# A prologue in finer steps, and a last projection by tiles, in a gated-attention and feed-forward kernel

## The chip, the cores and the metric

The kernel runs on one core of one Trainium2 chip. The metric is device time in microseconds (us), the median of some runs. A core has TensorE (PE, matrix products), VectorE (DVE), ScalarE (ACT), GpSimd (POOL) and SyncE (SP, which only starts transfers here). In the profile, matrix products show as MATMUL on PE with a weight load beside them (PEld); a product of fp32 operands shows as two instructions. PSUM, the memory that PE writes, has eight banks: ps_f has four and ps_a has four.

## The reference

16 sequences of 256 tokens, 256 wide, go through one layer of gated attention (an mLSTM in parallel form) and one feed-forward part of four layers.

```python
x = x + xattn(layernorm(x), ctx, ctx)      # q = normed x, k = v = ctx, 8 heads of 32
x = x + ffn(layernorm(x))

def xattn(q, k, v):
    pre = 15 * tanh((concat(q, k, v) @ ifgate_w.T + ifgate_b) / 15)     # 8 i-gates, 8 f-gates
    lf = cumsum(log_sigmoid(f_pre))
    log_d = lf[t] - lf[s] + i_pre[s], masked to t >= s;  m = rowmax(log_d)
    s_mat = (q k^T / sqrt(32)) * exp(log_d - m)
    h = s_mat v / (max(|rowsum(s_mat)|, exp(-m)) + 5e-5)
    return h * rsqrt(mean(h^2) + 1e-6) * (1 + outnorm_w)
def ffn(x):                                 # 256 -> 1024 -> 1024 -> 1024 -> 256, weights -1, 0, 1 with scales
    h = silu(x @ w1) * (x @ w2); h = gelu(h @ h1); h = gelu(h @ h2); return h @ w3
```

## The kernel before

The 16 sequences are worked through in 8 pairs (W = 2, so Q = 4 tiles of 128 tokens). A loop `batch(i)` on every engine does three things at once. It runs the feed-forward part of pair i. It runs the second half of the attention of pair j = i + 1 (masks, scores, values, residual, second norm). And it runs the first half for pair g = i + 2 (norm, turn, gates, scans). Each product of the feed-forward part is split into a high and a low part, so PE gets two passes (L1185 and L1186 for the first layer, L1209 and L1210 for the two hidden ones, L1242 and L1243 for the last).

What the loop overlaps has to be done in the open ahead of it: the whole attention of pair 0 and the first half of pair 1. This is the prologue, written out by hand at the end of each engine's program. Its order decides everything, since each engine takes its instructions in order and waits on semaphores. The steps, with the names that they have in the code:

- `norm_1_stats`, `norm_rsqrt`, `norm_1_apply` (DVE): mean and variance, then the root by integer seed and three Newton steps (eleven short linked instructions, L667 to L672), then z in four tiles (L693).
- `turn_z` (PE, L1036): 8 transposes of z into PSUM; `take_zT` (ACT, L510) copies them out.
- `plain_gates_keys` and `plain_gates_normed` (PE, L1059): gate products; `soft_cap` (tanh) and `softplus` (exp, ln) on ACT; between them an activation table is loaded (ACT_TABLE_LOAD).
- `scan_f`, `scan_m` (DVE): running sums and maxima over the 16 rows of gates. `spread_maxima` (PE, L1076) copies each of the 16 rows of maxima to all 128 partitions by a product that contracts over those 16 rows; `turn_rows` (L1106) turns the gate rows, `take_cols` (ACT) takes them out.
- `masks` (DVE, L776), `decays` (ACT, exp), `scores` (PE, L1128), `weigh_scores` (DVE, L792), `make_state` (L1137), `values` (PE, L1148: 8 heads of 33 columns each), `read_state` (L1158), `take_far`, `take_num`.
- `mix_divide`, `mix_square`, `mix_rsqrt`, `residual` (DVE), then the second norm (L678 to L693), `turn_z2` (L1036), `take_z2T` on ACT (z2_hi, L573) and on DVE (z2_lo, L872), and the first product of the feed-forward part (L1185).
- `keep_clock(n)` (PE, L1316) issues n products of no use, so that PE stays busy.

In the prologue the gates of pair 1 are worked out before pair 0's scores, with rows of pair 1 held in spare parts of z. POOL issues nine weight loads (11 MB), six ahead of `weigh_keys(0)` and three behind it. At the end `project` gives the last layer: two PSUM banks, each with both tiles of a sequence; `finish` (DVE) scales (L900) and adds (L906) a sequence at a time, and one transfer of 512 KB (L352) stores a pair. `decide` (L925) then sets a flag by which every engine skips a general path.

## Time and profile before

| | |
|---|---|
| median of 3 runs | 841.72 us (840.33 to 843.19) |
| the profiled execution's own time | 841.54 us |
| its span, first to last instruction | 839.7 us |
| PE busy, of the span | 97% |
| DVE, ACT, POOL busy | 66%, 45%, 6% |
| first feed-forward product starts | 80.94 us |
| last feed-forward product starts | 832.10 us |
| mean granted TensorE clock | 0.972 |

Times of instructions are us from the start of the span. The granted clock (PEclk) is 1.00 at 2.4 GHz and 0.50 at 1.2 GHz. A line of the timeline gives the start, the time that the merged instructions took, the engine, the line, the operation and the tiles, and in brackets the idle time before it and what ended it.

### The profile page before, as it was taken

The numbers are of one execution on the slowest core, as the hardware profiler recorded it, in microseconds if no ns is written. First come the engines' busy times: TensorE is split into PE (matmuls) and PEld (weight loads), VectorE is DVE, ScalarE is ACT, GpSimd is POOL, SyncE is SP. The second block draws the span as 40 slices with busy tenths as digits, with TensorE's granted clock in tenths as the row PEclk, the third lists the DMA queues.
The fourth block names the chain that finished last, engine by engine and source line by source line (L and its number), as shares of the span: only waits on it lengthen the run. The fifth ranks groups of instructions, "written<-read, shape, count | busy, mean of one in ns | idle before, by whom it ended". The sixth has DMA issues, their size and how long they took to land.

```text
span 839.7 us, 11914 instructions
## 1 busy us (share of the span) xinstructions
PE 816.1 (97%) x4666; PEld 693.7 (83%) x4666; DVE 558.1 (66%) x1335; ACT 375.9 (45%) x546; POOL 47.7 (6%) x53
## 2 busy tenths in 40 slices
PE   8895999999999999999999999999999999999996
PEld 7694788888888888888888888888888888888885
DVE  5656785758685695858666595947857583865543
ACT  2301554546345562455545462355535463336331
POOL 3100002000020001100020001100020000000000
PEclk9657999999999999999999999999999999999999
DMA  9804000040012200040002200131000300350540
GB/s 340 352 2 176 1 26 27 26 176 1 26 52 101 76 26 27 25 159 18 27 26 94 108 26 12 41 127 51 26 27 30 147 1 1 125 172 5 164 137 27
DMA packets 14027, 63.24 MB, mean 75 GB/s; under 512 B 1952, under 2 KB 2320, under 8 KB 11152
## 3 DMA queue, kind: packets, MB, share of 16 engines
q1 hardware_dynamic: 12672, 50.91, 17.4%
q0 software_dynamic: 1296, 11.53, 3.5%
q8 instruction: 38, 0.62, 0.3%
q14 instruction: 21, 0.17, 0.1%
HBM read 53.94 MB, written 8.50 MB: 74 GB/s over the span
## 4 chain that ended last, share of the span: by engine, by line
PE 78%; DVE 12%; issue 1%; ACT 1%; DVEq 0%; ACTq 0%
PE ps_f L1209 22%; PE ps_f L1210 22%; DVE decay L776 7%; PE ps_f L1185 7%; PE ps_f L1186 7%; PE ps_a L1148 6%; PE ps_f L1242 4%; PE ps_f L1243 4%; DVE decay L792 2%; PE ps_a L1128 2%; PE ps_a L1036 2%; PE ps_a L1137 1%; PE ps_a L1158 1%; PE ps_a L1099 1%; PE ps_a L1092 1%
## 5 line engine op out<-in xcount | busy, mean ns | idle before, releaser
L1209 PE MATMUL ps_f<-h_hi,wgt 128*128 128x512 f32 x1024 | 404.1, 395 | 0.0
L1210 PE MATMUL ps_f<-h_lo,wgt 128*128 128x512 f32 x1024 | 399.1, 390 | 0.0
L1209 PEld LDWEIGHTS ps_f<-h_hi,wgt 128*128 128x128 f32 x1024 | 192.4, 188 | 40.3 <-issue 0.5
L1210 PEld LDWEIGHTS ps_f<-h_lo,wgt 128*128 128x128 f32 x1024 | 192.4, 188 | 38.0
L890 DVE TENSOR_TENSOR h_lo<-work,h_hi 128x512 fp32r<-128x512 f32 x128 | 86.5, 690 | 135.0 <-ACT h_hi L596 134.0
L591 ACT ACTIVATE work<-ps_f,scl 128x512 f32<-128x512 f32 x128 | 87.5, 683 | 161.4 <-PE ps_f L1210 161.2
L1185 PE MATMUL ps_f<-h_hi,wgt 128*128 128x512 f32 x256 | 101.4, 396 | 0.1
L1186 PE MATMUL ps_f<-h_lo,wgt 128*128 128x512 f32 x256 | 100.4, 392 | 0.0
L578 ACT ACTIVATE work<-ps_f,scl 128x512 f32<-128x512 f32 x64 | 44.1, 688 | 92.6 <-PE ps_f L1186 92.6
L596 ACT ACTIVATE h_hi<-work 128x512 fp32r<-128x512 f32 x128 | 80.9, 632 | 4.0
L881 DVE SCALAR_TENSOR_TENSOR work<-ps_f,scl,work 128x512 f32<-128x512 f32 x64 | 48.1, 751 | 49.2 <-ACT work L578 49.2
L776 DVE SCALAR_TENSOR_TENSOR decay<-decay,cols,future 128x128 f32<-128x128 f32 x224 | 64.5, 364 | 0.0
L1242 PE MATMUL ps_f<-wgt,h_hi 128*128 128x256 f32 x256 | 62.2, 285 | 0.0
L1148 PEld LDWEIGHTS ps_a<-v_aug,decay 128*128 128x128 f32 x480 | 60.7, 201 | 1.6
L1243 PE MATMUL ps_f<-wgt,h_lo 128*128 128x256 f32 x256 | 61.8, 283 | 0.0
L1185 PEld LDWEIGHTS ps_f<-h_hi,wgt 128*128 128x128 f32 x256 | 48.0, 188 | 15.1 <-DVE work L881 3.7
L1148 PE MATMUL ps_a<-v_aug,decay 128*128 128x33 f32 x480 | 59.1, 280 | 0.0
L1186 PEld LDWEIGHTS ps_f<-h_lo,wgt 128*128 128x128 f32 x256 | 48.1, 188 | 8.8
L557 ACT ACTIVATE decay<-decay 128x1024 f32<-128x1024 f32 x32 | 33.9, 1060 | 42.8 <-DVE decay L776 42.8
L1243 PEld LDWEIGHTS ps_f<-wgt,h_lo 128*128 128x128 f32 x256 | 49.1, 192 | 0.1
L1242 PEld LDWEIGHTS ps_f<-wgt,h_hi 128*128 128x128 f32 x256 | 49.1, 192 | 0.1
L886 DVE TENSOR_TENSOR h_lo<-work,h_hi 128x512 fp32r<-128x512 f32 x64 | 43.7, 683 | 0.8
(156 smaller groups left out, 764.5 us busy)
## 6 DMA issues: line engine op xcount, KB each, us to landing
decay<-m_rows SPq DMA_DIRECT2D x14, 1024.0 KB, 6.1
decay<-w_cols SPq DMA_DIRECT2D x22, 512.0 KB, 4.2
wgt<-w_cols POOLq DMA_DIRECT2D x5, 1024.0 KB, 13.7
v_aug<-ctx_tok SPq DMA_DIRECT2D x8, 528.0 KB, 3.6
xs<-x SPq DMA_DIRECT2D x8, 512.0 KB, 3.6
wgt<-w_cols POOLq DMA_DIRECT2D x2, 2048.0 KB, 10.0
x_kept<-xs SPq DMA_DIRECT2D x8, 512.0 KB, 2.7
out<-xs SPq DMA_DIRECT2D x8, 512.0 KB, 2.6
```

What stands on the lines that cost most here:

```text
L591: act.activation(work[:, m % GELU], ps_f[:, (turn_of(i) + m) % 4], ACT.Gelu, scale=scl[:, 2 + layer, m:m + 1]).then_inc(s_gelu, 1)
L596: act.activation(h_hi[1 - layer][:, m], work[:, m % GELU], ACT.Copy).then_inc(s_hi, 1)
L776: last = dve.scalar_tensor_tensor(part, maxima, cols[:, t, row:row + 1], future[:], ALU.subtract, ALU.add)
L881: dve.scalar_tensor_tensor(work[:, 2 + m % 2], ps_f[:, bank], scl[:, 1, m:m + 1], work[:, m % 2], ALU.mult, ALU.mult).then_inc(s_hf, 1)
L890: dve.tensor_tensor(h_lo[1 - layer][:, m], work[:, m % GELU], h_hi[1 - layer][:, m].bitcast(F32), ALU.subtract).then_inc(s_lo, 1)
L1148: last = pe.matmul(value_out(j, b, t)[:, h * DV:(h + 1) * DV], decay_of(b, h, t), v_aug[:, b * TILES + t, h, :], start=True, stop=True)
L1185: pe.matmul(ps_f[:, bank + half], w, moving(z2_hi[:, c], as_is), start=(c == 0), stop=False)
L1186: last = pe.matmul(ps_f[:, bank + half], w, moving(z2_lo[:, c], as_is), start=False, stop=(c == CH - 1))
L1209: pe.matmul(ps_f[:, bank], w, moving(h_hi[layer][:, k], as_is), start=(k == 0), stop=False)
L1210: last = pe.matmul(ps_f[:, bank], w, moving(h_lo[layer][:, k], as_is), start=False, stop=(k == KH - 1))
L1242: pe.matmul(to, moving(h_hi[0][:, k, q * P:(q + 1) * P], as_is), w, start=(k == 0), stop=False)
L1243: last = pe.matmul(to, moving(h_lo[0][:, k, q * P:(q + 1) * P], as_is), w, start=False, stop=(k == KH - 1))
```

## The change

- First norms and turns of pair 0 go tile by tile: x comes in four transfers, each transposed tile follows its z tile, and the copies to zT, z2_hi and z2_lo are made in halves, which the gates and the first feed-forward products wait for one by one.
- The three roots of the prologue are exp(-0.5 ln v) on ACT (`root`), with one Newton step on DVE (`newton`), instead of eleven DVE steps.
- `spread_maxima` contracts over all 128 rows of state, cleared beforehand, and signals after each pair of heads.
- The values of a sequence are started when two of its four row groups are weighed (`first_values`). The second pair's turn, gates and scans come behind the first pair's values; `turn_rows(1)` and `take_cols(1)` come inside `batch(0)`.
- `split_gate_weights` and the gain go from DVE to POOL; gate_w and ctxT(0) are loaded from ACT's queue; two of the six weight loads that were ahead of `weigh_keys(0)` go behind it.
- The last pair's projection has a bank for each tile, and `finish_last` and `store_last` go by tiles.

```diff
+            for q in range(Q):
+                sp.dma_start(xs[0][:, q], x[0][:, q]).then_inc(s_x_first[q], 16)
...
+            def store_last(i):
+                for q in range(Q):
+                    b, t = q // TILES, q % TILES
+                    if t:
+                        sp.wait_ge(s_y, W * i + b + 1)
+                    else:
+                        sp.wait_ge(s_tail_y, b + 1)
+                    sp.dma_start(out[i][:, q], xs[i % 2][:, q]).then_inc(s_out if q == Q - 1 else s_tail_out[q], 16)
...
-            load_weights((0, 1, 2, 3, 4, 5))
+            load_weights((0, 1, 2, 3))
             weigh_keys(0)
-            load_weights((6, 7, 8))
+            load_weights((4, 5, 6, 7, 8))
+            split_gate_weights()
+            pool.wait_ge(s_gain, 16)
+            pool.tensor_scalar(gain_b[:], gain_b[:], 1.0, None, ALU.add).then_inc(s_gain, 1)
...
+            def root(n, logs, v, y):
+                act.wait_ge(s_var, n + 1)
+                act.activation(logs, v, ACT.Ln).then_inc(s_log, 1)
+                act.wait_ge(s_log, n + 1)
+                act.activation(y, logs, ACT.Exp, scale=-0.5).then_inc(s_root, 1)
...
+            act.dma_start(gw_in, gate_w).then_inc(s_gw, 16)
+            act.dma_start(ctxT(0), ctx_t[0]).then_inc(s_ctxT[0], 16)
+            act.preload_act_table_set("natural_log_exp_and_others")
+            root(0, nw[:, 1, 0:Q], nw[:, 0, 0:Q], nw[:, 3, 0:Q])
             act.preload_act_table_set("exp_and_others")
             take_zT(0)
             act.wait_ge(s_gb, 1)
             soft_cap(0)
+            act.wait_ge(s_cleared, 2)
             softplus(0)
-            act.preload_act_table_set("exp_and_others")
-            take_zT(1)
             take_cols(0)
             decay_cols(0)
             decays(0, 0)
+            decays(0, 1)
+            take_near(0)
+            take_zT(1)
+            root(1, rms[:, 1, 0:Q * HEADS], rms[:, 0, 0:Q * HEADS], rms[:, 3, 0:Q * HEADS])
+            act.preload_act_table_set("exp_and_others")
             soft_cap(1)
-            decays(0, 1)
             softplus(1)
-            take_near(0)
-            take_cols(1)
-            act.wait_ge(s_layer_const, 32)
+            root(2, nw[:, 1, 0:Q], nw[:, 0, 0:Q], nw[:, 3, 0:Q])
+            act.preload_act_table_set("silu_and_others")
             take_z2T(0)
+            act.wait_ge(s_scl, 16)
...
+            def newton(tile, n):
...
+                link(s_lead, 0, dve.tensor_tensor(prod, y, y, ALU.mult))
+                link(s_lead, 0, dve.scalar_tensor_tensor(prod, prod, -0.5, v, ALU.mult, ALU.mult))
+                link(s_lead, 0, dve.scalar_tensor_tensor(y, prod, 1.5, y, ALU.add, ALU.mult))
+            def first_norm_stats(src, landed):
+                for q in range(Q):
+                    if landed:
+                        dve.wait_ge(s_x_first[q], 16)
+                    last = dve.bn_stats(stats[:, q], src[:, q])
+                link(s_lead, 0, last)
+                for q in range(Q):
+                    last = dve.bn_aggr(mv[:, q], stats[:, q])
+                link(s_lead, 0, last)
+                dve.tensor_scalar(nw[:, 0, 0:Q], mv[:, :, 1], LN_EPS, None, ALU.add).then_inc(s_var, 1)
+            def first_norm_apply(root, src, dst, done):
+                dve.wait_ge(s_root, root + 1)
+                newton(nw, Q)
+                for q in range(Q):
+                    dve.tensor_scalar(dst[:, q], src[:, q], mv[:, q, 0:1], nw[:, 3, q:q + 1], ALU.subtract, ALU.mult).then_inc(done, 1)
+                dve.wait_ge(done, Q)
...
+            def first_num(b):
+                if b == 0:
+                    dve.wait_ge(s_gw_split, 4)
+                dve.wait_ge(s_far, 1)
+                dve.wait_ge(s_pv, TILES * (b + 1))
+                dst = num[:].rearrange("p (b t e) -> p b t e", b=W, t=TILES)[:, b, 1]
+                far = state[:].rearrange("p (b n) -> p b n", b=W)[:, b]
+                added = dve.tensor_tensor(dst, value_out(0, b, 1), far, ALU.add)
+                if b:
+                    added.then_inc(s_num, 1)
+                    dve.wait_ge(s_num, 1)
+                else:
+                    link(s_lead, 0, added)
+            def first_square(b):
+                n = TILES * HEADS
+                at = slice(b * n, (b + 1) * n)
+                sq = h_sq.rearrange("p (n d) -> p n d", d=DH)[:, at]
+                if b:
+                    dve.wait_ge(s_near, 1)
+                else:
+                    dve.wait_ge(s_near_first, 1)
+                link(s_lead, 0, dve.tensor_tensor(sq, heads[:, at, 0:DH], heads[:, at, 0:DH], ALU.mult))
+                link(s_lead, 0, dve.tensor_reduce(rms[:, 2, at], sq, AX.X, ALU.add))
+            def first_mix():
+                total = heads[:, :, DH]
+                dve.wait_ge(s_floor, 1)
...
+                dve.tensor_scalar(rms[:, 0], rms[:, 2], RMS_EPS, None, ALU.add).then_inc(s_var, 1)
+                dve.wait_ge(s_root, 2)
+                newton(rms, Q * HEADS)
+                link(s_lead, 0, dve.tensor_tensor(den[:, 0], rms[:, 3], den[:, 1], ALU.mult))
...
+            def finish_last(i):
+                for q in range(Q):
+                    b, t = q // TILES, q % TILES
+                    at, bank = slice(t * DIM, (t + 1) * DIM), (turn_of(i) + q) % 4
+                    dve.wait_ge(s_ymm, Q * i + q + 1)
+                    scaled = dve.tensor_tensor(y_tmp[:, b, at], ps_f[:, bank, 0:DIM], w3s_b[:], ALU.mult)
+                    if t:
+                        scaled.then_inc(s_ysc, 1)
+                        dve.wait_ge(s_ysc, W * i + b + 1)
+                    else:
+                        scaled.then_inc(s_tail_scaled, 1)
+                        dve.wait_ge(s_tail_scaled, b + 1)
+                        dve.wait_ge(s_x1kept, 16 * i + 16)
+                    kept = resident(i)[:, q]
+                    dve.tensor_tensor(kept, y_tmp[:, b, at], kept, ALU.add).then_inc(s_y if t else s_tail_y, 1)
...
-            norm_1_stats(0)
-            norm_rsqrt(s_norm1, 0)
-            norm_1_apply(0)
+            dve.memset(state[:, 0:2 * SEQ], 0.0).then_inc(s_cleared, 1)
+            first_norm_stats(xs[0], True)
+            first_norm_apply(0, xs[0], z, s_z_first)
             dve.wait_ge(s_const, 16)
             dve.tensor_scalar(gb[:], gb_in[:], 1.0 / CAP, None, ALU.mult).then_inc(s_gb, 1)
             norm_1_stats(1)
             norm_rsqrt(s_norm1, 1)
+            scan_f(0)
+            shift_g(0)
+            scan_m(0)
             norm_1_apply(1)
-            scan_f(0)
-            scan_m(0)
             dve.wait_ge(s_ident, 8)
-            masks(0)
+            masks(0, (0,))
+            masks(0, (1,), (0,))
             weigh_scores(0, 0)
+            masks(0, (1,), (1,))
+            floors(0)
+            take_state(0)
             weigh_scores(0, 1)
-            take_state(0)
+            take_far(0)
+            first_num(0)
+            first_square(0)
+            first_num(1)
+            first_square(1)
+            assert count[s_lead] == LEAD_REDUCED, count[s_lead]
+            first_mix()
+            residual(0)
+            first_norm_stats(xs[0], False)
             scan_f(1)
-            scan_m(1)
-            split_gate_weights()
-            floors(0)
-            dve.wait_ge(s_gain, 16)
-            dve.tensor_scalar(gain_b[:], gain_b[:], 1.0, None, ALU.add).then_inc(s_gain, 1)
-            take_far(0)
-            take_num(0)
-            mix_divide(0)
-            mix_square(0)
-            mix_rsqrt(0)
-            residual(0)
-            norm_2_stats(0, xs[0])
-            norm_rsqrt(s_norm2, 0)
-            norm_2_apply(0, xs[0])
+            first_norm_apply(2, xs[0], z2, s_z2_first)
+            shift_g(1)
+            running_max(1)
             take_z2T(0)
-            dve.wait_ge(s_layer_const, 32)
+            offsets(1)
+            dve.wait_ge(s_scl, 16)
...
+            def turn_first(src, ready, half_done, done):
+                for q in range(Q):
+                    pe.wait_ge(ready, q + 1)
+                    for c in range(CH):
+                        last = pe.transpose(ps_a[:, c, q * P:(q + 1) * P], src[:, q, c * P:(c + 1) * P], ident[:])
+                        if q == Q - 1:
+                            last.then_inc(done if c else half_done, 1)
...
-            def spread_maxima(b, heads_of):
-                for h in heads_of:
+            def spread_maxima(b, h0):
+                for h in (h0, h0 + 1):
                     row = b * HEADS + h
-                    last = pe.matmul(spread_out(h), ident[0:BH, row:row + 1].to_broadcast([BH, P]), m_row(0),
+                    last = pe.matmul(spread_out(h), ident[:, row:row + 1].to_broadcast([P, P]), state[:, SEQ:2 * SEQ],
                                      start=True, stop=True)
-                return last
+                last.then_inc(s_spread, 1)
...
+            def first_values(b, part):
+                pe.wait_ge(s_smat, ROWGRP * b + 2 * part + 2)
+                for r in FIRST_WEIGHED[2 * part:2 * part + 2]:
+                    for h in (r, r + ROWGRP):
+                        for t in range(TILES):
+                            last = pe.matmul(value_out(0, b, t)[:, h * DV:(h + 1) * DV], decay_of(b, h, t), v_aug[:, b * TILES + t, h, :],
+                                             start=True, stop=True)
+                last.then_inc(s_pv, 1)
...
+                    if first(i) and m == 2:
+                        turn_rows(1)
...
-            keep_clock(20)
+            keep_clock(14)
             plain_gates_keys(0)
+            turn_first(z, s_z_first, s_zT_first, s_zT)
+            keep_clock(2)
+            plain_gates_normed(0)
+            keep_clock(18)
+            pe.wait_ge(s_scan, 3)
+            pe.wait_ge(s_cleared, 2)
+            spread_maxima(0, 0)
+            turn_rows(0)
+            for h in (2, 4, 6):
+                spread_maxima(0, h)
+            pe.wait_ge(s_mask, 1)
+            for h in (0, 2):
+                spread_maxima(1, h)
+            scores(0, 0)
+            pe.wait_ge(s_mask, 2)
+            for h in (4, 6):
+                spread_maxima(1, h)
+            pe.wait_ge(s_v, 16)
+            first_values(0, 0)
+            make_state(0)
+            first_values(0, 1)
+            scores(0, 1)
+            read_state(0)
+            first_values(1, 0)
+            first_values(1, 1)
+            turn_z(1)
             plain_gates_keys(1)
-            turn_z(0)
-            plain_gates_normed(0)
-            keep_clock(8)
-            turn_z(1)
-            keep_clock(8)
-            pe.wait_ge(s_scan, 3)
+            plain_gates_normed(1)
+            keep_clock(24, 1)
             pe.wait_ge(s_zTe, 2)
-            spread_maxima(0, range(0, 2))
-            pe.wait_ge(s_cleared, 1)
-            turn_rows(0)
-            spread_maxima(0, range(2, 4)).then_inc(s_spread, 1)
-            spread_maxima(0, range(4, 8)).then_inc(s_spread, 1)
-            pe.wait_ge(s_mask, 1)
-            spread_maxima(1, range(0, 4)).then_inc(s_spread, 1)
-            plain_gates_normed(1)
-            pe.wait_ge(s_mask, 2)
-            spread_maxima(1, range(4, 8)).then_inc(s_spread, 1)
-            scores(0, 0)
-            scores(0, 1)
-            make_state(0)
-            values(0, 0, 0)
-            values(0, 1, 0)
-            read_state(0)
-            values(0, 0, 1)
-            values(0, 1, 1)
-            turn_rows(1)
-            keep_clock(24, 1)
-            turn_z2(0)
-            keep_clock(8, 1)
+            turn_first(z2, s_z2_first, s_z2T_first, s_z2T)
+            keep_clock(2, 1)
```

## Rows read from the trace of the kernel before

**Rows 1.** Windows: busy us (instructions) of PE, PEld, DVE, ACT, POOL; granted clock; DMA; GB/s.
```profile
82.00:176.00 94.00, 93.91 (x549) 79.75 (x548) 65.15 (x157) 47.58 (x69) 6.19 (x4) 1.00 0.11 40
```
**Rows 2.** Timeline, first norm, turn and gates of pair 0.
```profile
2.12 7.49 PE L1316 MATMUL ps_f<-ident 128*128 128x128 f32 x40 [2.12 <-POOL ident L469]
8.73 1.38 DVE L693 TENSOR_SCALAR z<-xs,mv,nw 128x256 f32<-128x256 f32 x4
...
15.33 1.93 PE L1059 MATMUL ps_a<-work,num 128*48 128x256 f32 x8 [1.11 <-ACT work L510]
```
**Rows 3.** Timeline, table load, exp and running sum of the first gates.
```profile
17.85 1.28 ACT L531 ACT_TABLE_LOAD   x1
...
19.14 0.42 ACT L535 ACTIVATE state<-rows 16x256 f32<-16x256 f32 x1
...
20.11 0.68 DVE L743 TENSOR_TENSOR_SCAN state<-state 16x256 f32<-16x256 f32 x1 [4.28 <-ACT state L537]
```
**Rows 4.** Timeline, maxima spread, masks, scores weighed, values.
```profile
23.80 7.75 PE L1076 MATMUL ps_f<-state,ident 16*128 16x256 f32 x20
...
25.08 2.37 DVE L776 SCALAR_TENSOR_TENSOR decay<-ps_f,cols,future 128x128 f32<-128x128 f32 x8 [2.17 <-PE ps_f L1076]
...
39.24 2.47 DVE L792 SCALAR_TENSOR_TENSOR decay<-ps_a,decay 128x512 f32<-128x512 f32 x4
...
47.59 0.46 DVE L718 MEMSET gw_split<- 128x480 f32 x1 [0.16 <-issue]
...
52.34 6.88 PE L1148 MATMUL ps_f<-v_aug,decay 128*128 128x33 f32 x32
```
**Rows 5.** Windows cut where the granted clock changes; columns as in the first group.
```profile
22.40:25.00 2.60, 2.51 (x12) 1.91 (x13) 0.47 (x2) 0.65 (x3) 0.33 (x1) 1.00 1.07 433
25.00:31.40 6.40, 6.40 (x16) 4.54 (x14) 4.41 (x16) 2.08 (x2) 2.47 (x5) 0.50 0.85 313
31.40:35.10 3.70, 3.70 (x10) 1.49 (x9) 2.16 (x8) 0.03 (x1) 0.00 (x0) 0.50 1.06 443
...
46.00:50.00 4.00, 4.00 (x20) 4.00 (x21) 2.85 (x14) 0.39 (x1) 0.00 (x0) 0.50 0.02 4
...
62.50:66.50 4.00, 3.93 (x35) 3.74 (x34) 3.52 (x15) 0.00 (x0) 0.00 (x0) 0.99 0.49 164
```
**Rows 6.** Chain that ended last, batch 0: the attention steps amid the feed-forward part.
```profile
111.87 1.17 PE ps_a L1128 x32
...
120.53 0.90 PE ps_a L1137 x8
121.43 1.71 PE ps_a L1148 x16
```
**Rows 7.** Chain that ended last, from the mixing's root to the first feed-forward product.
```profile
64.23 0.19 DVE rms L667
...
66.92 1.24 DVE num L856
...
70.70 1.42 DVE stats L678 x4
...
76.38 1.98 PE ps_a L1036 x8
...
78.44 1.03 ACT h_hi L573
...
79.57 1.24 DVE h_lo L872
...
80.94 0.47 PE ps_f L1185
```
**Rows 8.** The page's transfers: KB each, us from issue to landing.
```profile
decay<-m_rows SPq DMA_DIRECT2D x14, 1024.0 KB, 6.1
```
**Rows 9.** Timeline, the end.
```profile
832.42 0.69 DVE L900 TENSOR_TENSOR num<-ps_f,w3s_b 128x512 f32<-128x512 f32 x1 [1.22 <-PE ps_f L1243]
833.03 1.28 DVE L906 TENSOR_TENSOR xs<-num,xs 128x512 f32<-128x512 f32 x2
...
834.34 0.34 SPq L352 DMA_DIRECT2D out<-xs  x1
```

More of the change, by code:

```diff
@@ L216, in build @@
         s_out = sem("s_out")
+        s_tail_scaled = sem("s_tail_scaled")
+        s_tail_y = sem("s_tail_y")
+        s_tail_out = [sem(f"s_tail_out{n}") for n in range(Q - 1)]
         def first(j):
             return isinstance(j, int) and j == 0
-        def early(j):
-            return isinstance(j, int) and j == 1
         def zT(j):
@@ L394, in _ @@
                         load_raw(n)
-                store(i)
+                    store_last(i)
+                else:
+                    store(i)
+            for n in range(Q - 1):
+                sp.wait_ge(s_tail_out[n], 16)
             sp.wait_ge(s_x1kept, 16 * PAIRS)
@@ L526, in soft_cap @@
                     act.wait_ge(s_gate_sum, j - W + 1)
-                act.activation(rows[0:GATE_COLS], gate_out(j)[0:GATE_COLS] if plain(j) else gate_sum, ACT.Tanh, bias=gb[:], scale=1.0 / CAP).then_inc(s_gact, 1)
+                act.activation(rows[0:GATE_COLS], gate_out[0:GATE_COLS] if plain(j) else gate_sum, ACT.Tanh, bias=gb[:], scale=1.0 / CAP).then_inc(s_gact, 1)
             def softplus(j):
@@ L603, in batch @@
                         hi_1(i, m - 1)
+                    if first(i) and m == 3:
+                        take_cols(1)
                 hi_1(i, KH - 1)
@@ L756, in scan_m, with offsets @@
                 dve.wait_ge(s_scan, n + 3)
+            def offsets(j):
+                f, m = f_row, m_row
+                g = rows[ROW_G:ROW_G + BH]
                 c = m[:, P - 1:P]
@@ L787, in weigh_scores @@
             def weigh_scores(j, b):
-                for r in range(ROWGRP):
+                for r in FIRST_WEIGHED if first(j) else range(ROWGRP):
                     dve.wait_ge(s_qk, W * j + b + 1)
@@ L1244, in part @@
                     return last
+                if final:
+                    for t in range(TILES):
+                        part(0, t, range(KH - 1))
+                    for t in range(TILES):
+                        part(0, t, range(KH - 1, KH)).then_inc(s_ymm, 1)
+                    for t in range(TILES):
+                        part(1, t, range(KH)).then_inc(s_ymm, 1)
+                    return
                 for b in range(W):
```

238 lines of the change are left out of this document (148 added, 90 removed).

## The prediction, made before the changed kernel ran

> **What bounds the kernel now.** I read the page first: one core, PE busy 97% of the span. The windows cut to stretches then say where PE isn't the bound. In a stretch inside the loop PE is busy 93.91 of 94 us at the full clock [rows 1], and the edits hardly touch it. So the change can pay only before the first feed-forward product, at 80.94 [rows 7], and behind the last product of the projection, at 832.1. What lies between is fixed: from 80.94 to the span's end 758.8 us, and 1.8 us more in the execution's own time of 841.5, which is 0.2 us under the median.
>
> The first 80.94 us are a chain through four engines. Three parts of it matter. (1) Up to the gates of pair 0, PE is in the way: 40 products of no use until 9.6, then the key gates, and the gates on normed x end at 17.26 [rows 2]. (2) From 25.1 to 59.2 it is masks, scores and values, and here the granted clock decides. It is 1.00 when the spread of maxima begins and 0.50 from 25.0 [rows 5]. PE is busy without a break from 25.0 to 31.4 with products that contract over 16 rows, and the clock does not come back. It comes back at 35.1, after 3.7 us of gate products over 128 rows [rows 5]. So rows in use count, and busy time alone doesn't. It is low again through the values, where PE is likewise never idle (46 to 50), and high again from 62.5 under useless 128-column products [rows 5]. The price: 16 value instructions take 1.71 us in the loop [rows 6], 32 take 6.88 us here [rows 4], so 3.44 for 16, double. (3) From the last values (59.2) to 80.94 DVE works alone, step by step [rows 7].
>
> **The change, part by part.**
>
> *First gates.* 28 useless instructions take the place of 40. At their mean of 0.187 us they end at 7.4, and at the slower rate of their start near 8.1; I take 8.0. Then 1.93 for the key gates, 1.0 for 8 transposes (1.98 at half clock [rows 7]), so the turn ends at 11.0. The z tiles are no longer in the way: they were ready at 10.1 [rows 2] and come about 1.7 earlier by the short root and the four transfers of x. Half copies of 0.55 (1.03 for the whole [rows 7]) let the first half of the gate products start at 11.6, so they end at 13.6: 3.7 us earlier. Two transfers more on SP's queue and two on ACT's cost some 0.4 each at the start, where these queues have nothing else. The bound on the other side: if the clock rises later, the key gates cost 1.9 more.
>
> *Gates to masks.* Tanh, table load, exp and ln stay as they are: running sum at 20.11 before [rows 3], 16.45 now. The maximum is ready 1.85 later (18.3), offsets 0.9, and `norm_1_apply(1)` (1.4) now stands between them and the masks. Masks start at 20.65, not at 25.08.
>
> *Masks, scores, values.* DVE's work, with eight masks at 2.2 and a weighing at 2.47 [rows 4]: 4.35 for sequence 0, 2.2, weighing 2.5 (ends 29.7), 2.2, floors and state 0.95, weighing 2.5. At full clock PE keeps up: a pair of heads spread in 0.9 (1.9 for 5 instructions at half clock, 7.75 for 20 [rows 4]), so DVE never waits long. The first values start at 28.45, when two row groups are weighed. They take 1.71, state 0.90, values 1.71, scores 1.17 to 1.5 [rows 6], and DVE weighs sequence 1 until 36.85. The last values end at **39.1**. That is the floor. But in this stretch PE has 33-column products and gaps, much as where the clock was low before. What I expect is that the spread, now over 128 rows, holds the clock (as the gate products brought it back), and that it falls amid the first values, near 32. Then the second values, scores, state and last values run at half clock: second values until 33.9, scores 36.0, state read 38.1, two values of 3.44 each until **45.0**. If it falls at 28.4, the last values end at **48.6**. If the 128 rows don't help and it is low from 22 on, every spread pair costs 1.7, masks wait as before, and they end at **53.8**.
>
> *Last values to first feed-forward product* (21.7 us before). Half of the squares is hidden (1.25 off). The mix's root: eleven DVE steps at 0.224 (twelve fill 64.23 to 66.92 [rows 7]), 2.46, become ln and exp on ACT and three steps. No row has a 128x4 or 128x32 ln; below lies 0.4 for both, above the 0.42 each of a 16x256 exp plus three handovers of 0.1 [rows 3], 1.2. I take 0.65, nearer the small end since the elements are few: 1.1 off. The second norm's root is the same, but `scan_f(1)` (0.68) lies in it: 0.9 off. The turn of z2 follows the tiles, at full clock: 1.98 becomes 0.5, 1.5 off. z2_hi (1.03) and z2_lo (1.24) go in halves, the second halves beside the first products, with `running_max(1)` 0.25 in the way: 1.2 off [rows 7]. Sum 6: **15.4 to 15.9** us remain.
>
> What is moved behind the values is pair 1: turn, gates (2 x 1.93 at full, double at half clock), useless products, then on ACT tanh, two table loads, exp, ln. At full clock they are ready 7.7 us after the last values, where DVE wants them at 10.7. If the clock is low they need 9.5 to 12, and `scan_f(1)` and the ACT root behind it wait up to 1.4. That is inside the 15.9.
>
> By the Trainium skill, "ScalarE: Activation LUTs", section "What ACT_TABLE_LOAD costs", a switch takes about 2.66 us, 1.28 of load and 1.38 of drain. Here the load starts at 17.85, takes 1.28, and exp starts at 19.14 [rows 3], so no such drain stands behind it. By the page's figure the second gates would be ready 2.8 us later, and the time would be an estimated 823.5. The sum goes by the row.
>
> *Moved to POOL.* `split_gate_weights` and the gain: DVE had a gap there (memset 0.46 at 47.59 [rows 4]), so nothing is gained, and POOL does them from about 24.5, ahead of the first read at 33. Nothing; at most 1.6 (their time on DVE) if they stood in DVE's way.
>
> *Moved into batch 0.* `turn_rows(1)` on PE and `take_cols(1)` on ACT: 0.5 us on the bound engine. The copy of maxima (6.1 us [rows 8]) has 19 us before the masks of batch 0: hidden. Cost **+0.5**.
>
> *The end.* Before: scale 832.42, two adds, store at 834.34 [rows 9]. The last product ends at the same time. Now a half scale (0.4) and a half add (0.35): store at 833.3. 1.0 off, and 0 to 1.2 for a quarter of the bytes; I take **1.3 off**.
>
> **Sum.** 45.0 + 15.9 = 60.9 for the first product, 20.0 earlier; 841.5 - 20.0 + 0.5 - 1.3 = 820.7, so **821**.
>
> **Rivals.**
> - *The clock holds through the values.* Products start at 39.1 + 15.4 = 54.5, at most 1 us lost if it falls in the pause before the turn: 841.5 - 26.4 + 0.5 - 1.3 = 814.3, or 815. For it: the loop has such values at full clock [rows 1, 6], though among big products. Against: they didn't bring the clock back in 46 to 50 [rows 5]. Chance 0.20.
> - *The clock is low from the start of values, or the second gates come late on top:* 48.6 + 15.8 = 64.4, so 824.2. For it: more pauses in PE than before. Chance 0.22.
> - *The change doesn't do what it says:* the spread over 128 rows counts no more than one over 16, the clock falls near 22. 53.8 + 15.7 = 69.5: 829.3. For it, the rows added hold zeros; against it, the 48-column gate products that brought the clock back. Chance 0.12.
> - *Slower: weights.* Loads 4 to 8 (14 of 22 units of 0.52 MB, 7.3 MB) now stand behind `weigh_keys(0)`, which waits for columns, shortly ahead of the masks at 20.65. Issued from some 21.8, at the lowest busy rate of 313 GB/s [rows 5] they land by 45; the second layer needs its first ones at 60.9 + 15 = 76. Each us beyond that is a us lost; it decides from a landing at 96 (100 GB/s). Against it: 31 us of room. Chance 0.03, for this and what I don't see.
> - *A drain behind each table load.* If a pause as long as a load (1.28) stood behind each of the two loads of the second gates, they would be 2.6 later and the first product with them: 820.7 + 2.6 = 823.3. Against it: exp starts 0.01 us after the load [rows 3]. Chance 0.02. This is the drain of the Trainium skill's "ScalarE: Activation LUTs", named above.
> - *No change:* the same mechanism just at 96. Chance 0.01.
>
> The forecast itself has 0.40. A measurement of this kernel tells 0.3% (2.5 us) from no change; faster 0.96, same 0.01, slower 0.03. The range goes from the case of the holding clock to near the failed one, with 2 us for the unknown roots and the store: **813 to 828**.
>
> **What would show it.** Right: gates of pair 0 end near 13.6; masks start near 20.7; PEclk 1.00 under the spread and 0.50 somewhere in the values; last values near 45; first feed-forward product near 61; store near 1 us after the last scale starts. Wrong: PEclk 0.50 in the spread; DVE waiting for the second gates; PE at the end of the useless products after z2 is ready; layer two waiting for a load.

## The result, and the profile after

| | before | after |
|---|---|---|
| median of the compared runs, us | 842.46 (840.33 to 843.36, 4 runs) | 813.69 (812.77 to 814.21, 4 runs) |
| profiled execution: own time, span, us | 841.54, 839.7 | 814.18, 812.3 |
| first feed-forward product, us | 80.94 [rows 7] | 54.20 |
| last projection product, us | 832.10 | 806.27 |

The ratio is 0.9657, with an interval of 0.9637 to 0.9677: 28.8 us faster. The time lies inside the range of the prediction (813 to 828) and 7.3 us under its forecast of 821. It is the time of the rival in which the clock holds through the values (814.3), which had a chance of 0.20.

The loop is what it was: in 94 us from the middle of batch 0 PE is busy 93.89, at the full clock, against 93.91 [rows 1]. The stretches ahead of it answer to [rows 5]. Columns: busy us and instructions of PE, PE's weight loads, DVE, ACT, POOL; granted clock; DMA share; GB/s.

```profile
24.00:30.00 6.00, 5.60 (x62) 4.62 (x61) 6.00 (x19) 2.11 (x2) 2.42 (x8) 1.00 1.08 439
30.00:34.90 4.90, 4.70 (x64) 4.34 (x62) 2.98 (x10) 1.45 (x2) 0.00 (x0) 1.00 1.03 431
34.90:37.60 2.70, 2.59 (x23) 2.59 (x24) 2.58 (x6) 0.00 (x0) 0.00 (x0) 1.00 1.07 443
37.60:39.80 2.20, 2.20 (x13) 2.20 (x13) 1.10 (x2) 0.03 (x1) 0.00 (x0) 0.50 0.97 384
148.00:242.00 94.00, 93.89 (x546) 79.63 (x545) 65.91 (x159) 45.77 (x68) 6.20 (x4) 1.00 0.13 45
```

The clock is at its full level through the spread and the masks, where it was at half before, and through nearly all values. It falls only at 37.6, when 2.2 us of values are left, and rises again at 44.4. The timeline of the prologue, for [rows 2 to 4]:

```profile
7.68 1.93 PE L1234 MATMUL ps_a<-work,w3s_b 128*48 128x256 f32 x8
...
8.52 1.38 DVE L773 TENSOR_SCALAR z<-xs,mv,nw 128x256 f32<-128x256 f32 x4
...
11.21 1.93 PE L1234 MATMUL ps_a<-work,w3s_b 128*48 128x256 f32 x8
...
13.73 1.28 ACT L584 ACT_TABLE_LOAD   x1
...
15.03 0.42 ACT L590 ACTIVATE state<-rows 16x256 f32<-16x256 f32 x1
...
19.03 2.79 PE L1254 MATMUL ps_f<-state,ident 128*128 128x256 f32 x12
...
20.23 6.29 DVE L871 SCALAR_TENSOR_TENSOR decay<-ps_f,cols,future 128x128 f32<-128x128 f32 x24
...
26.44 2.48 DVE L887 SCALAR_TENSOR_TENSOR decay<-ps_a,decay 128x512 f32<-128x512 f32 x4
...
27.87 1.94 PE L1323 MATMUL ps_a<-v_aug,decay 128*128 128x33 f32 x16 [0.40 <-DVE decay L887]
...
33.67 2.48 DVE L887 SCALAR_TENSOR_TENSOR decay<-ps_f,decay 128x512 f32<-128x512 f32 x4 [1.92 <-PE ps_f L1304]
...
35.01 4.73 PE L1323 MATMUL ps_f<-v_aug,decay 128*128 128x33 f32 x32 [0.31 <-DVE decay L887]
```

Twelve spread instructions take 2.79 us, so 0.23 each, where the twenty of before took 7.75, 0.39 each. 24 masks take 6.29, so 0.26 each back to back, where the first eight of before took 2.37 plus 2.17 of waiting for the spread. DVE sets the pace now, and PE follows it.

The chain that ended last, from the mixing's root to the first feed-forward product, for [rows 7]:

```profile
43.32 0.24 ACT rms L629
...
44.75 1.24 DVE num L986
...
48.53 1.42 DVE stats L762 x4
...
50.55 0.58 DVE state L827
...
51.99 1.06 DVE num L773 x3
...
54.24 0.70 DVE h_lo L1004
...
54.98 0.50 PE ps_f L1374
```

The end, in the timeline, for [rows 9]:

```profile
806.59 0.42 DVE L1053 TENSOR_TENSOR num<-ps_f,w3s_b 128x256 f32<-128x256 f32 x1 [1.04 <-PE ps_f L1433]
807.04 0.42 DVE L1062 TENSOR_TENSOR xs<-num,xs 128x256 f32<-128x256 f32 x1
```

**The sum of the measured pieces.** The last projection product comes 25.83 us earlier (832.10 to 806.27). From there to the span's end it is 6.03 us against 7.60, so 1.57 less. 841.54 - 25.83 - 1.57 = 814.14, against 814.18 measured. Of the 25.83, the first feed-forward block explains all but 0.1: its first product starts 26.74 earlier, but the first blocks wait for halves, and the third block starts 4.50 us behind the first product against 3.71 before. The start that is comparable is therefore 54.99 (54.20 plus the difference of 0.79), 25.95 earlier.

### The profile page after: what moved, and what is told of

It is laid out like the page before. It is cut to its first block, busy times and chain, and to the rows that moved or that the text cites. A ratio compares the mean times of both kernels' runs of the same rounds, so it can differ in the third digit from the quotient of the medians.

```text
span 812.3 us, 11892 instructions
## 1 busy us (share of the span) xinstructions
PE 801.1 (99%) x4650; PEld 678.9 (84%) x4650; DVE 554.2 (68%) x1311; ACT 378.6 (47%) x555; POOL 50.4 (6%) x61
## 4 chain that ended last, share of the span: by engine, by line
PE 82%; DVE 14%; ACT 2%; issue 1%; POOL 0%; DVEq 0%; POOLq 0%; ACTq 0%
PE ps_f L1397 23%; PE ps_f L1398 22%; DVE decay L871 8%; PE ps_f L1371 7%; PE ps_f L1374 7%; PE ps_a L1332 6%; PE ps_f L1432 4%; PE ps_f L1433 4%; DVE decay L887 2%; PE ps_a L1304 2%; PE ps_a L1198 1%; PE ps_a L1313 1%; PE ps_a L1342 1%; PE ps_f L1517 1%; PE ps_a L1277 1%
## 5 line engine op out<-in xcount | busy, mean ns | idle before, releaser
L1332 PEld LDWEIGHTS ps_a<-v_aug,decay 128*128 128x128 f32 x448 | 53.8, 192 | 1.6
L1332 PE MATMUL ps_a<-v_aug,decay 128*128 128x33 f32 x448 | 52.3, 272 | 0.0
```

Source lines behind the costliest of these rows:

```text
L1332: last = pe.matmul(value_out(j, b, t)[:, h * DV:(h + 1) * DV], decay_of(b, h, t), v_aug[:, b * TILES + t, h, :], start=True, stop=True)
```

## The experiments

No kernel here leaves out a part of the computation. "After" is the changed kernel, 813.69 us.

**What holds the clock: rows in the spread.** Undo one part: the spread contracts over the 16 rows in use again, nothing else.

```diff
-    ident[:, row:row + 1].to_broadcast([P, P]), state[:, SEQ:2 * SEQ]
+    ident[0:BH, row:row + 1].to_broadcast([BH, P]), state[0:BH, SEQ:2 * SEQ]
```

> The changed kernel with one edit undone: the maxima are spread by products that contract over 16 rows again, not over 128. Theory (rows in use keep the clock up): the granted clock falls to 0.50 within the spread or soon after it, before 28 us, stays there through the values, the last values end at 48 to 54 us instead of 39.7, and the time is 822 to 829 us. Rival (busy PE is what counts, and the new order alone keeps PE busy): the clock holds until the last values and the time stays at 813 to 815 us.

Measured: 822.23 us (821.24 to 822.92), ratio to before 0.9766 (0.975 to 0.9783); 8.5 us slower than after. Windows of this kernel, cut where its clock changes:

```profile
18.00:21.90 3.90, 3.67 (x15) 2.89 (x16) 3.76 (x14) 0.65 (x3) 1.46 (x3) 0.91 0.65 245
21.90:31.80 9.90, 9.90 (x52) 7.78 (x50) 8.27 (x27) 3.17 (x3) 4.91 (x13) 0.50 0.96 371
31.80:44.60 12.80, 12.80 (x81) 12.38 (x81) 4.08 (x12) 1.45 (x2) 0.00 (x0) 0.50 0.70 288
44.60:48.60 4.00, 4.00 (x35) 4.00 (x35) 3.13 (x6) 0.06 (x1) 0.00 (x0) 0.93 0.00 0
```
```profile
44.60 3.91 PE L1323 MATMUL ps_f<-v_aug,decay 128*128 128x33 f32 x32
```

PE is busy 9.90 of 9.90 us, and the clock is at half all the same. It stays there for the first values and the second scores as well. At 45.0 it comes back, under the last 32 value instructions, which take 3.91 at the full clock; no row shows why there and not sooner. They end at 48.5 and not at 39.74, and the first product starts at 62.96. The instructions differ from those of after in the rows of the spread alone, so the rows hold the clock through the spread, though 112 of them hold zeros.

The same part alone, put into before:

```diff
-    ident[0:BH, row:row + 1].to_broadcast([BH, P]), m_row(0)
+    ident[:, row:row + 1].to_broadcast([P, P]), state[:, SEQ:2 * SEQ]
+            dve.memset(state[:, 0:2 * SEQ], 0.0).then_inc(s_cleared, 1)
```

> The kernel before with one part of the change alone: the spread contracts over 128 rows of a cleared state. Theory (rows): the clock stays at 1.00 through the spread, the masks end some 5 to 8 us earlier, and if the clock falls only in the values the time is 828 to 836 us. Rival (the order of steps is what pays, not the clock): the time stays within 3 us of the kernel before, 839 to 843 us.

Measured: 834.75 us (828.66 to 837.66, 6 runs), ratio 0.9911 (0.9878 to 0.9945): 6.9 us faster than before (841.66 in these rounds). Its timeline:

```profile
24.88 6.41 DVE L777 SCALAR_TENSOR_TENSOR decay<-ps_f,cols,future 128x128 f32<-128x128 f32 x24 [2.25 <-PE ps_f L1078]
...
45.91 6.88 PE L1150 MATMUL ps_f<-v_aug,decay 128*128 128x33 f32 x32
```

The clock is full until 40.0 in the profiled run, so the masks run at 0.27 each. Then it falls, 1.4 us after the first values began (PE had waited 1.31 us just ahead of them and their state product), and the last 32 values take 6.88 as before [rows 4]. This is the forecast's picture, hold in the spread and fall in the values, in the old order of work. In the new order it was wrong.

**What the pause ahead of the values does.** After begins the first values when two of four row groups are weighed. Here they wait for all four.

```diff
-                pe.wait_ge(s_smat, ROWGRP * b + 2 * part + 2)
+                pe.wait_ge(s_smat, ROWGRP * b + ROWGRP)
```

> The changed kernel, but each sequence's values wait until all four row groups of its scores are weighed, not two. Theory (the first half of the values is hidden behind the weighing, and PE is what DVE waits for at the last values): the last values end 1.2 to 2.5 us later and the time is 815 to 817 us. Rival (DVE's own work covers it, or the clock holds longer and gives it back): 813 to 814.5 us.

Measured: 821.32 us (819.68 to 822.34), ratio 0.9745 (0.9723 to 0.9768): 7.6 us slower than after, where the delay alone was expected to cost 1.2 to 2.5. Windows and timeline of this kernel:

```profile
26.00:31.80 5.80, 4.20 (x28) 3.67 (x29) 5.57 (x18) 1.41 (x2) 1.00 (x2) 0.99 1.05 436
31.80:47.90 16.10, 15.55 (x95) 14.95 (x95) 5.62 (x9) 1.09 (x2) 0.00 (x0) 0.50 0.57 232
```
```profile
29.49 1.94 PE L1323 MATMUL ps_a<-v_aug,decay 128*128 128x33 f32 x16 [1.60 <-DVE decay L887]
...
40.91 7.04 PE L1323 MATMUL ps_f<-v_aug,decay 128*128 128x33 f32 x32 [0.55 <-DVE decay L887]
```

The wait of 0.40 ahead of the values is now 1.60, the clock falls at 31.7 and stays low until about 51, and the last values end at 47.95. This is the clock case of the forecast, place and price (fall near 32, 5 us and more). Its cause is either the pause or the later place. So the pause was filled: the same kernel, with seven useless 128-column products ahead of the first values.

```diff
             pe.wait_ge(s_v, 16)
+            pe.wait_ge(s_mask, 3)
+            keep_clock(7, 0)
             first_values(0, 0)
```

> The values of a sequence wait for all four row groups, as in the run of that name, which took 821.3 us with the clock at 0.50 from 31.9 us on; and now seven useless products of 128 columns stand in PE's pause of 1.6 us ahead of the first values. Theory (the pause, not the later start, let the clock fall): the clock holds at 1.00 until 36 us or later, only the later start of the values is left as a cost, and the time is 814.5 to 817 us. Rival (the longer run of 33-column products lowers it, whatever stands ahead of them): the clock falls near 32 us again and the time is 820 to 822 us.

Measured: 816.53 us (815.33 to 818.53), ratio 0.9687 (0.9665 to 0.9709). Windows of this kernel:

```profile
26.00:39.00 13.00, 11.49 (x116) 10.75 (x111) 9.95 (x26) 2.63 (x4) 1.15 (x3) 0.99 1.03 424
39.00:44.00 5.00, 5.00 (x25) 5.00 (x25) 1.38 (x2) 0.00 (x0) 0.00 (x0) 0.50 0.42 165
```

The first values start as late as in the kernel without the filling (29.54), yet the clock holds until 38.8 and the last values end at 44.2, in a profiled execution (818.53) that is the slowest of the four. Some 4.8 of the 7.6 us come back in the medians; the delay itself costs 2.8 at most. So it is the idle time ahead of the values, and not their late place, that let the clock fall. The second pause of this kernel, 1.51 us ahead of sequence 1's values at 37.91, was left unfilled, and the clock falls 0.9 us behind it. (Whether the same pause filled with other work than 128-column products would do as much wasn't tried.)

**Does the run of 32 value instructions end the hold?** In the profiled run of after the clock falls amid it. Here sequence 1's values are parted by five useless products.

```diff
             first_values(1, 0)
+            pe.wait_ge(s_smat, 2 * ROWGRP)
+            keep_clock(5, 0)
             first_values(1, 1)
```

> The changed kernel with five useless products of 128 columns (one more wait, for the last weighing, ahead of them) between the halves of sequence 1's values. In the changed kernel the clock falls at 37.6 us, amid that run of 32 value instructions. Theory (a run of 33-column products alone lets it fall): it holds at 1.00 through the values; the products cost 1.1 us and the clock gives 0.9 back, so the last values end at 39.5 to 40.2 us, the second gates come 2 to 3 us earlier and the time is 813 to 815 us. Rival (the fall has another cause): the clock falls near 37 to 38 us all the same, the last values end at 41 or later, and the time is 815 to 817 us.

Measured: 814.52 us (814.1 to 815.49), ratio 0.9678 (0.9656 to 0.9701). The clock is full through the values, which end at 40.2. It falls near 53.9, behind the turn of z2, and the first products run at 0.63 to 0.79 us each for a while. PE had waited 2.4 us ahead of that turn, but so it did in three other kernels (the second run without the 18 products, 20 useless products, the last version) in which the clock stayed up there. It doesn't tell the theories apart: the clock held over the same 32 instructions in four other kernels without such products too (the second run without the 18 products, 20 useless products in place of 14, the integer roots, and the last version below; 3.76 us for the 32 in each). What ends the hold at 37.6 in one run stays open. Its price can be read: these 32 take 4.73 in the profiled run of after, so 1.0 more. Two of after's four runs list a clock of 0.998 and 812.8 and 813.2 us, the other two, of which one is the profiled, 0.994 and 814.2. A kernel whose profiled execution kept the clock there has to be compared with that 1.0 us in mind.

**The 18 useless products in the pause of the gates.** They stand between the gates of pair 0 and the spread.

```diff
-            keep_clock(18)
```

> The changed kernel without the 18 useless products between the first gates and the spread, so that PE idles from 13 to 17.9 us. Theory: the clock falls to 0.50 near 18 us; the products over 128 rows bring it back while the spread runs, so the loss is 1 to 4 us: 815 to 818 us. Rival (nothing but the useless products keeps the clock up, the 128 rows don't): it stays at 0.50 through the values and the time is 822 to 829 us.

Measured: 816.67 us (815.8 to 817.03), ratio 0.9702 (0.9686 to 0.9718). Windows of this kernel:

```profile
13.00:17.40 4.40, 0.00 (x0) 0.00 (x0) 2.60 (x9) 2.47 (x4) 0.00 (x0) 0.84 1.04 385
17.40:21.20 3.80, 3.67 (x10) 2.94 (x11) 3.11 (x11) 0.65 (x3) 0.53 (x1) 0.50 0.86 331
21.20:24.50 3.30, 3.30 (x14) 2.73 (x13) 2.80 (x12) 1.06 (x1) 3.30 (x7) 0.76 0.47 117
24.50:28.00 3.50, 3.50 (x44) 2.84 (x43) 3.50 (x14) 1.62 (x2) 2.54 (x9) 1.00 1.10 440
```

PE does nothing for 4.4 us and the clock falls. It is back at 1.00 under the spread over 128 rows by 24.5, which is the forecast's claim that these rows also raise it. The first product starts at 54.10 and the span is 812.2, against 812.3 in after. That doesn't mean that the fall is free. The first gates end 0.3 sooner here (12.79), yet sequence 1's values start 0.9 later (35.89), so the fall costs 1.2; the clock then holds nearly through them (3.76 us against after's 4.73), which gives 1.0 back. And the own time is 4.46 us above the span, where after has 1.9. The kernel was run again to see whether that repeats.

> The same kernel as in the run without the 18 useless products, once more. That one had a span as long as the changed kernel's (812.2 us) and yet took 816.7 us, 4.5 us outside the span where all others had 1.8 to 1.9. Theory (something of the program's start or end outside the span depends on it): 816 to 817 us again, with a span near 812. Rival (a matter of that chip or hour): 814 us.

Measured: 817.16 us (817.02 to 817.75), ratio 0.9699; span 813.1 and 4.65 us outside it. It repeats: in the eight runs of the two, 4.0 to 4.65 us lie outside, in after's four 1.9 to 2.0. Sequence 1's values start at 36.97, with gates that end 0.3 later than after's, so here the fall costs 1.6. The 18 products are worth 1.2 to 1.6 us ahead of the values and some 2.4 (between the medians) outside the span. No row shows what the second part is; it is left open.

**The roots.** After, with its three roots by eleven DVE steps each in place of ln and exp on ACT.

```diff
-                dve.tensor_scalar(nw[:, 0, 0:Q], mv[:, :, 1], LN_EPS, None, ALU.add).then_inc(s_var, 1)
-                dve.wait_ge(s_root, root + 1)
-                newton(nw, Q)
+                link(s_lead, 0, dve.tensor_scalar(nw[:, 0, 0:Q], mv[:, :, 1], LN_EPS, None, ALU.add))
+                rsqrt(s_lead, 0, nw, Q)
```

> The changed kernel with its three prologue roots by eleven DVE steps again instead of ln and exp on ACT and one Newton step. Theory (DVE alone works from the last values to the first feed-forward product): the root of the mix costs 1.2 us more and that of the second norm 0.9 to 1.1, the first norm's 0.5 to 1.1, so the first feed-forward product starts 2.5 to 3.3 us later and the time is 816 to 817 us. Rival (the roots lie beside the second gates and the scan, and cost nothing): 813 to 814.5 us.

Measured: 818.18 us (817.96 to 819.3), ratio 0.9727 (0.971 to 0.9743), 4.5 slower than after and 1.2 above the time expected. From the mixing's add to its quotient it is 2.92 us against 1.64, so +1.3. The second norm, from the add to the first tile of z2, is 2.95 against 1.28, so +1.7, of which 0.6 is the running sum: it stands ahead of DVE's root here, and in after it runs beside ACT's. The values of sequence 1 start 1.5 later (36.48), but 0.6 of that is x, which landed later in this execution (statistics end at 7.41, not 6.80). The clock held through the values here, so only 0.5 of the 1.5 is left when they end, and it fell at 55.2 in the pause before the turn, so the turn takes 1.94 where after's takes 1.31, and the first product comes another 0.5 later. These four (0.5, 1.3, 1.7, 0.5) are 4.0, the first product's delay (58.17 against 54.20); the two spans differ by 3.8. Rows of this kernel:

```profile
46.52 1.22 DVE L981 TENSOR_TENSOR num<-num,den 128x1024 f32<-128x1024 f32 x1
...
55.10 1.38 DVE L769 TENSOR_SCALAR num<-xs,mv,nw 128x256 f32<-128x256 f32 x4
...
55.66 1.94 PE L1210 MATMUL ps_a<-ident,num 128*128 128x128 f32 x8 [5.38 <-DVE num L769]
```

**The first useless products, 20 in place of 14** (two instructions each): the bound of the first gates from the side of PE.

```diff
-            keep_clock(14)
+            keep_clock(20)
```

> The changed kernel with 20 useless products ahead of the first gates, as before, not 14. Theory (PE's queue is in the way of the first turn): the first gates end 1.0 to 1.3 us later and the time is 814.7 to 815.2 us. Rival (the z tiles are in the way): 813.2 to 814.2 us.

Measured: 814.95 us (814.19 to 815.25), ratio 0.967 (0.9649 to 0.9691), 1.3 slower. The key gates start at 9.72 and not at 7.68, and the gates of pair 0 end at 15.18, 2.0 later. Sequence 1's values start 2.0 later too:

```profile
37.04 3.76 PE L1323 MATMUL ps_f<-v_aug,decay 128*128 128x33 f32 x32 [0.31 <-DVE decay L887]
```

The first product comes only 1.05 later, at 55.25, since the clock is full through the whole prologue here and the 32 value instructions take 1.0 less than in after's profiled run. Against after's two runs that list the same clock of 0.998 (812.8 and 813.2) the median is 1.9 slower, so the two us of PE are on the chain in full. The rival, that the z tiles are in the way, is out.

**The four transfers of x.** After, with x of pair 0 in one transfer, and the gate weights and keys' columns from SP's queue behind it.

```diff
-            for q in range(Q):
-                sp.dma_start(xs[0][:, q], x[0][:, q]).then_inc(s_x_first[q], 16)
+            sp.dma_start(xs[0][:], x[0]).then_inc(s_x_first[0], 16)
+            sp.dma_start(gw_in, gate_w).then_inc(s_gw, 16)
+            sp.dma_start(ctxT(0), ctx_t[0]).then_inc(s_ctxT[0], 16)
```

> The changed kernel with the first loads as before: x of pair 0 in one transfer, then the gate weights and the turned context, all from one queue. Theory (the four transfers of x beside the context land later than one, 6.8 us for the end of the statistics against 5.8 before, and the turn of z waits for the last z tile): the statistics end near 5.8 us, the first gates end 0.2 to 0.5 us earlier or at the same time, and the time stays within 0.5 us, 813 to 814.5 us. Rival (early tiles pay): 814.5 to 816 us.

Measured: 813.6 us (812.16 to 814.72), ratio 0.9657 (0.9635 to 0.9679): the same as after. Timeline of this kernel:

```profile
4.32 1.40 DVE L761 BATCH_NORM_STATS2 stats<-xs 128x6 f32<-128x256 f32 x4 [2.57 <-DMA xs<-x]
...
9.87 1.09 PE L1214 MATMUL ps_a<-ident,z 128*128 128x128 f32 x8
```

The statistics end at 5.72, a us before those of after (6.80; 5.78 in before). But the tiles of z wait, since PE is in the key gates until 9.94. So x by tiles gains nothing; it lands later as a whole (the statistics end at 6.80 to 7.41 in the runs of after, 20 useless products, the parted values and the integer roots), and PE's work hides nearly all of it. The context's columns come from another queue in this run, so the later landing isn't shown to come from the four transfers alone.

**The tail alone**, put into before: `finish_last`, `store_last` and the last projection by halves.

> The kernel before with the end of the change alone: the last projection with a bank for each tile, finished and stored by tiles. Theory: the last product ends at the same time, the last store is issued 1.0 us earlier and lands up to 1 us sooner, so the span is 1.3 to 2.2 us shorter: 840 to 841 us beside 842.5. Rival (the skip of the general path, and not the store, ends the span): 0.5 us or less.

Measured: 840.68 us (838.68 to 843.04, 10 runs) against 842.33 (13 runs), ratio 0.9983 (0.9967 to 0.9999): 1.65 us. It is under the 0.3% that a measurement tells from no change, though the interval just leaves 1 out. In both profiles the piece from the last product to the span's end shrinks by about as much (1.5 here, 1.57 in after), and the last add is a half one:

```profile
832.48 0.42 DVE L939 TENSOR_TENSOR xs<-num,xs 128x256 f32<-128x256 f32 x1
```

**A version from what was learned:** after with x in one transfer, 12 first useless products in place of 14, the gain of sequence 0 multiplied while DVE waits for the state, and the second pair's maximum behind the split of z2.

```diff
-            shift_g(1)
-            running_max(1)
-            take_z2T(0)
+            take_z2T(0)
+            shift_g(1)
+            running_max(1)
             offsets(1)
```

> The changed kernel with four small edits that the rows point to: x of pair 0 in one transfer, so that z is ready earlier; 12 useless products ahead of the first gates, not 14; sequence 0 of pair 0 multiplied by the gain in DVE's wait for the last values; shift_g(1) and running_max(1) behind the split of z2 and not ahead of it. Theory: 0.4 us of the first gates, 0 to 0.6 of the gain and 0.2 of the split lie on the chain, so the first feed-forward product comes 0.6 to 1.3 us earlier and the time is 812.4 to 813.2 us. Rival (a phase of the clock or the later pair 1 takes it back): 813.5 to 815 us.

Measured: 812.64 us (812.25 to 813.06, 5 runs), ratio 0.966 (0.9646 to 0.9675) to a before of 841.29. The first product starts at 52.17 (2.0 earlier) in a span of 809.9, with the clock full throughout the prologue; half of the 2.0 is the 1.0 that the clock costs after's profiled run in the last values. The median is 1.05 under after's, but the two ratios' intervals overlap, so it isn't shown to beat it.

## Why the prediction was right, and where it was off

Right: the sign, the size within the range, and where the change could pay. The loop is unchanged, and the gain lies ahead of the first feed-forward product (26) and at the end (1.6). Off: the case taken as the likeliest, with a chance of 0.40; the range reached the measured time only because its lower end was laid at the rival in which the clock holds. The step that failed is "that it falls amid the first values, near 32". The clock held until 37.6, and the last values ended at 39.74, where the step gave 45.0 and its rival's floor 39.1. That is 5.3 of the 6.6 us between the sum (820.7) and the profiled execution's 814.2. The step drew on the values of before, which didn't bring a low clock back [rows 5]. With whole row groups they don't either (31.8 to 47.9), though with the spread over 16 rows it came back amid them, at 45.0. But to keep a full clock is another thing than to raise a low one, and what decided it was PE's pause ahead of the values: 0.40 us in after and the clock stays over the first 32 and some more, 1.60 us with whole row groups and it falls just where the forecast had it, the same pause filled with products and it stays until 1.51 us of pause ahead of the last values. Why it falls at 37.6 in after's profiled run, behind a pause of 0.31 us, isn't shown. The change starts the values on two row groups, and the prediction used that for its time (28.45) but not for the clock.

By steps:

- *Rows in use hold the clock.* Shown from both sides: without them after loses 8.5 us, with them alone before gains 6.9. Without the 18 products the low clock even rises under the spread. The rival that the rows don't help was put at 829.3; the kernel in which they are gone took 822.23, so that rival's last values (53.8) were too late by 5.3 us. They ended at 48.5. Of this 3.0 is the last 32 values, which ran at the full clock (3.91, where at half they take 6.88 [rows 4]); the rival had it low to their end.
- *First gates.* Forecast 13.6 for the end of pair 0's gates, measured 13.14 (11.21 + 1.93). The useless products end by 7.68, not 8.0. "The z tiles come 1.7 earlier" failed in its reason: the statistics ended 1.0 later (6.80), the short root won it back, and the tiles ended at 9.90, 0.2 earlier than before. PE left the key gates at 9.61 and turned tile after tile without a gap. The run with x in one transfer shows that it didn't matter.
- *Masks start* 20.23 (forecast 20.65), *first values* 27.87 (28.45), *weighing of sequence 1* ends at 36.15 (36.85): all by the 0.45 of the gates, and 0.25 more by masks of 0.26.
- *Last values to first product.* 15.25, forecast 15.4 to 15.9, of which the sum took the larger. Against before it is 6.5 less, where the terms sum to 6: the mix up to its add 1.4 (1.25 forecast), the mixing's root 1.3 (1.1), the second norm's root 1.1 (0.9), the turn and the halves of z2 2.7 (2.7). The 1.7 of the roots' experiment isn't the term of 0.9: it has the running sum in it, which before doesn't have there.
- *Second gates in time.* They are ready at 49.21, and DVE takes them at 50.46 for the running sum. No wait.
- *No drain behind the table load.* The load at 13.73 takes 1.28, so ends at 15.01, and exp starts at 15.03. The rival with a drain (823.3) is out by that row and by the time. The Trainium skill, "ScalarE: Activation LUTs", section "What ACT_TABLE_LOAD costs", has 1.38 us of drain beside the load's 1.28; this trace shows it neither ahead of the load (tanh ends at 13.71) nor behind it, and the measurement decides.
- *Weights.* Hidden: the DMA share is near 1 from 24.0 to 39.8 at 384 to 443 GB/s, and from the first blocks to the last projection product the two kernels differ by 0.1 us. The same 0.1 bounds `turn_rows(1)` and `take_cols(1)` in batch 0 (forecast 0.5): they are hidden too, or nearly, unless something else in batch 0 got shorter.
- *POOL's work.* Nothing, as forecast: the 24 masks beside it run at 0.26 each.
- *The end.* 1.57, forecast 1.3. The store of 128 KB lands in 1.7 us, that of 512 KB took 2.6.

The misses add up: 5.3 for the end of the values, 0.65 from there to the first product, 0.4 in batch 0 and 0.3 at the end make 6.6, the difference of 820.7 and 814.1.

## What to carry to other kernels

A fallen clock is paid on everything behind it, so a small pause of PE ahead of thin products can be worth far more than its length: starting the values 1.6 us later cost 7.6, and 4.8 of it came back when the pause was filled. Give thin products to PE as soon as their first part is ready, and let products that only spread a row contract over all rows, if the others are zero. When two kernels are compared by one profiled execution each, look whether the clock fell in one of them and not in the other: that alone was 1.0 us here, half of what 20 useless products cost. Before splitting a load to start earlier, look at who is really last: four tiles of x won nothing, since PE was in the key gates.

## What the runs showed of the hardware that was not expected

- With the spread over 16 rows PE is busy 9.90 of 9.90 us at a granted clock of 0.50 (1.2 GHz); with the same instructions over 128 rows, 112 of them zeros, the clock is 1.00 (2.4 GHz), and in the kernel without the 18 products it came back from 0.50 to 1.00 under them.
- 33-column products over 128 rows can keep a full clock (3.76 us for 32 of them, in five profiled executions). A stretch of 16.1 us with 48 of them, in which PE was busy 15.55, ran at half clock to its end; with the spread over 16 rows the clock came back from 0.50 to 1.00 amid them, at 45.0, PE having been busy without a break since 21.9. What makes the difference isn't known.
- Where PE paused 1.3 to 1.6 us just ahead of such products, or of the state product before them, the clock fell 0.9 to 2.4 us after PE resumed (three times, in three kernels); with 0.40 us or none it held over the first 32 in nine executions of the changed kernel and its relatives.
- The time outside the span isn't a constant: 4.0 to 4.65 us in the eight runs without the 18 useless products at 13 us, against 1.9 to 2.0 with them and 1.7 to 2.4 in all other kernels here. No row shows why.
- ln and exp over 128x32 elements take 0.23 us each on ACT, with a handover of 0.03 between them: from the add at 43.11 to the quotient at 44.75 it is 1.64 us.
- The same bytes in four transfers of 128 KB, with others beside them, were all there at least 1.1 us later than in one, by the end of the statistics.
